# A graph network on one core: each gather asks SyncE and waits for its answer to the one before

## The reference

```python
h = relu(layernorm(x)); x = x + L0(h)   # 4 heads: softmax over a node's edges of (k[src]*q[dst]), typed weights, 8 edge types
h = relu(layernorm(x)); x = x + L1(h)   # GAT: softmax of leaky_relu(a_src[src] + a_dst[dst]), then a feed-forward part
h = relu(layernorm(x)); x = x + L2(h)   # graph convolution: agg = segment_sum(h[src], dst)
h = relu(layernorm(x)); x = x + L3(h)   # 8 heads: exp(clip(k[src]*q[dst], -5, 5)), sums over dst, a feed-forward part
```

## Time and profile before

| | us |
|---|---|
| median of 3 runs (lowest, highest) | 12209.15 (12207.96, 12222.4) |
| profiled execution, its own time | 12230.88 |
| its span in the trace | 12229.1 |
| windows taken for the four passes | 534 to 3580, 3774 to 6710, 6922 to 9181, 9340 to 12070 |

### The profile page before, as it was taken

One profiled execution on the slowest core, in us unless ns is written; L12 is line 12 of the kernel. 1 busy time (PEld: TensorE's weight loads), 2 busy tenths in 40 slices (PEclk: granted clock), 3 DMA queues, 4 the chain that ended last, 5 costly groups with the idle time before them and its releaser, 6 DMA issues. The chain is left out here.

```text
span 12229.1 us, 162378 instructions
## 1 busy us (share of the span) xinstructions
PE 7123.3 (58%) x41810; PEld 5769.1 (47%) x41811; DVE 4523.4 (37%) x12921; ACT 2930.1 (24%) x7688; POOL 6254.5 (51%) x6407
## 2 busy tenths in 40 slices
PE   5766666666665555555555433333335666666667
PEld 3555555555553444444444333222233555555555
DVE  4244444444454444444444411111113333333334
ACT  1233333333333333333333300000002211212112
POOL 1244444444543555555554466666663555555552
PEclk9866566665666555555555655556555665666667
DMA  3322222222221111111111122222222222222221
GB/s 116 134 69 66 68 70 67 69 70 68 69 61 41 38 37 38 38 37 38 37 38 36 42 46 46 46 46 47 46 46 64 76 76 74 77 77 76 75 76 49
DMA packets 379359, 730.33 MB, mean 60 GB/s; under 512 B 169738, under 2 KB 219201, under 8 KB 372838
## 3 DMA queue, kind: packets, MB, share of 16 engines
q0 software_dynamic: 251264, 621.88, 19.5%
q1 hardware_dynamic: 100474, 96.66, 2.4%
q10 hardware_dynamic: 27500, 10.39, 0.4%
HBM read 651.60 MB, written 76.88 MB: 60 GB/s over the span
## 5 line engine op out<-in xcount | busy, mean ns | idle before, releaser
L461 POOL DMA_INDIRECT edges_rows<-kv_typed,edges_idx_r x1568 | 1505.5, 960 | 1584.1 <-DVE edges_wv L781 1103.1
L461 POOL DMA_INDIRECT edges_rows<-gat_rows,edges_idx_r x1568 | 1523.3, 971 | 1421.3 <-DVE edges_wv L781 985.6
L461 POOL DMA_INDIRECT edges_rows<-kv_rows,edges_idx_r x1568 | 1516.6, 967 | 1237.5 <-DVE edges_wv L1145 775.7
L461 POOL DMA_INDIRECT edges_rows<-conv_rows,edges_idx_r x1568 | 1544.5, 985 | 777.0 <-issue 456.9
L609 PE MATMUL edges_ps_sum<-edges_wv,edges_pick 128*128 128x132 f32 x7040 | 1733.5, 417 | 96.5 <-issue 91.0
L985 PE MATMUL edges_ps_sum<-edges_rows,edges_pick 128*128 x3520 | 768.1, 356 | 1516.9 <-issue 1388.5
L609 PEld LDWEIGHTS edges_ps_sum<-edges_wv,edges_pick 128*128 128x128 f32 x7040 | 1466.0, 302 | 268.6 <-issue 246.8
L985 PEld LDWEIGHTS edges_ps_sum<-edges_rows,edges_pick 128*128 128x128 f32 x3520 | 648.9, 258 | 1636.1 <-issue 1634.5
L1083 PE MATMUL edges_ps_q<-q,edges_pick_t 128*128 x3520 | 799.1, 401 | 918.7 <-ACT edges_pick_t L1121 727.8
L1083 PEld LDWEIGHTS edges_ps_q<-q,edges_pick_t 128*128 128x128 f32 x3520 | 728.9, 305 | 968.5 <-issue 968.5
L591 PE MATMUL edges_ps_q<-q,edges_pick_t 128*128 x3520 | 821.9, 409 | 563.9 <-ACT edges_pick_t L696 429.5
(11 more groups left out here) (344 smaller groups left out, 11299.7 us busy)
## 6 DMA issues: line engine op xcount, KB each, us to landing
kv_typed<-l0pre_out SPq DMA_DIRECT2D x49, 1024.0 KB
edges_rows<-kv_typed,edges_idx_r POOLq DMA_INDIRECT x1568
edges_rows<-gat_rows,edges_idx_r POOLq DMA_INDIRECT x1568
edges_rows<-conv_rows,edges_idx_r POOLq DMA_INDIRECT x1568
edges_rows<-kv_rows,edges_idx_r POOLq DMA_INDIRECT x1568
edges_feat_r<-visit_features ACTq DMA_DIRECT2D x660, 10.0 KB
kv_rows<-l3pre_kv SPq DMA_DIRECT2D x7, 896.0 KB, 4.0
edges_flag_r<-visit_flags ACTq DMA_DIRECT2D x220, 16.0 KB
```

Source lines behind the costliest of these rows:

```text
L461: pool.indirect_dma_start(rows[:, k, g * width:(g + 1) * width], None, table, bass.IndirectOffsetOnAxis(ap=idx_r[:, k, g:g + 1], axis=0)). ...
```

## The change

Two semaphores are new, `asked` and `answered`; `slot_free` is gone. Ahead of every gather but the first of a pass POOL waits until `answered` has counted the gather before, and counts `asked` up; the gather follows. SP's stream now runs over the same groups as POOL's, and for each gather waits for `asked` and counts `answered` up. POOL counts `asked` for gather n and issues it without waiting for the answer to n; it is gather n+1 that waits for that. The index lists are loaded from the same loop of SP, after the second group of every 7 (`k % HALF == 1`), with a wait for `rows_ready` of one group more than before.

```diff
-def supply(sp, idx, idx_r, idx_in, rows_ready):
+def supply(sp, idx, idx_r, idx_in, rows_ready, asked, answered):
...
     for n in range(2):
         load(n * HALF, n)
-    with sp.bass.Fori(1, NGP // SLOTS, engines=only(sp), hint_back_edge=True) as it:
-        for n in range(2):
-            sp.wait_ge(rows_ready, (it - 1) * SLOTS + (n + 1) * HALF)
-            load(it * SLOTS + n * HALF, n)
+
+    def body(j, k, it):
+        for g in range(G):
+            sp.wait_ge(asked, j * G + (g + 1))
+            sp.sem_inc(answered, 1)
+        if k % HALF == 1 and known(j, HALF) and (not isinstance(j, int) or j + SLOTS - 1 < NGP + HALF):
+            sp.wait_ge(rows_ready, j - 1)
+            load(j - 1 + HALF, (k // HALF + 1) % 2)
+    groups(sp, body)
...
         if known(j, SLOTS):
             pool.wait_ge(used, at_least_one(pool, visits[k % HALF], NV))
-        pool.sem_inc(slot_free, 1)
         for g in range(G):
+            if g or known(j, 1):
+                pool.wait_ge(answered, j * G + g)
+            pool.sem_inc(asked, 1)
             pool.indirect_dma_start(rows[:, k, g * width:(g + 1) * width], None, table,
                                     bass.IndirectOffsetOnAxis(ap=idx_r[:, k, g:g + 1], axis=0)).then_inc(rows_in[k], 16)
```

More of the change, by code:

```diff
@@ L441, in supply, with fetch @@
         load(n * HALF, n)
-    with sp.bass.Fori(1, NGP // SLOTS, engines=only(sp), hint_back_edge=True) as it:
-        for n in range(2):
-            sp.wait_ge(rows_ready, (it - 1) * SLOTS + (n + 1) * HALF)
-            load(it * SLOTS + n * HALF, n)
-def fetch(nc, pool, res, rows, table, width, idx_r, idx_in, rows_in, rows_ready, used, slot_free):
+    def body(j, k, it):
[6 more added lines that the diff above has]
+    groups(sp, body)
+def fetch(nc, pool, res, rows, table, width, idx_r, idx_in, rows_in, rows_ready, used, asked, answered):
     visits = []
@@ L513, in softmax_pass @@
         rows_in, idx_in = [p.sem(f"rows_in{k}") for k in range(SLOTS)], [p.sem(f"idx_in{k}") for k in range(2)]
-        rows_ready = p.sem("rows_ready")
-        (slot_free, zeroed, squares_done, pick_t_done, pick_tb_done, pick_b_done, pick_done, q_done, prod_done, edge_done,
+        rows_ready, asked, answered = (p.sem(n) for n in ("rows_ready", "asked", "answered"))
+        (zeroed, squares_done, pick_t_done, pick_tb_done, pick_b_done, pick_done, q_done, prod_done, edge_done,
          logit_done, turn_done, run_done, back_done, ends_done, ends_high, ends_low, marked, restarted, top_part, absent_done,
@@ L529, in _ @@
                     sp.dma_start(source[:], idx.rearrange("p g t -> p (g t)")).then_inc(source_in, 16)
-                supply(sp, idx, idx_r, idx_in, rows_ready)
+                supply(sp, idx, idx_r, idx_in, rows_ready, asked, answered)
             @block.gpsimd
             def _(pool):
-                fetch(nc, pool, res, rows, table, width, idx_r, idx_in, rows_in, rows_ready, wv_done, slot_free)
+                fetch(nc, pool, res, rows, table, width, idx_r, idx_in, rows_in, rows_ready, wv_done, asked, answered)
             @block.tensor
@@ L947, in conv_pass @@
         rows_in, idx_in = [p.sem(f"rows_in{k}") for k in range(SLOTS)], [p.sem(f"idx_in{k}") for k in range(2)]
-        rows_ready, slot_free = p.sem("rows_ready"), p.sem("slot_free")
+        rows_ready, asked, answered = (p.sem(n) for n in ("rows_ready", "asked", "answered"))
         local_in, pick_done, sum_done, acc_done = (p.sem(n) for n in ("local_in", "pick_done", "sum_done", "acc_done"))
@@ L963, in _ @@
                 sp.dma_start(local[:], dram["local"]).then_inc(local_in, 16)
-                supply(sp, idx, idx_r, idx_in, rows_ready)
+                supply(sp, idx, idx_r, idx_in, rows_ready, asked, answered)
             @block.gpsimd
             def _(pool):
-                fetch(nc, pool, res, rows, table, aw, idx_r, idx_in, rows_in, rows_ready, sum_done, slot_free)
+                fetch(nc, pool, res, rows, table, aw, idx_r, idx_in, rows_in, rows_ready, sum_done, asked, answered)
             @block.tensor
```

2 lines of the change are left out of this document (1 added, 1 removed).

## The result

The changed kernel takes 12,647.4 us (median of 4 runs, 12,598.5 to 12,656.9) against 12,215.2 for the kernel before: a ratio of 1.0346, 95% interval 1.0317 to 1.0374. Forecast were 11,524 us and a gain.

The account below looks back on a forecast made before the run. Long runs of gathers holding up other engines' signals and sequencers, not work, were taken to bound the passes. 6272 gathers at 1.64 us plus 1258 us gave 11,544, 685 below the span; off the median, 11,524 us, range 10,300 to 12,900.

Parts of the forecast that it names:

- That signals are held while gathers run: In the four edge passes, back-to-back gathers delay other engines' semaphore updates; ACT's L696 waits 1261.8 us in the first pass.
- the prediction's formula: Time is 1258 us outside the edge passes plus 6272 gathers times the time per gather; break-even at 1.749 us.
- POOL slows exactly when signals are held: In the edge passes SP's late answers stop POOL, held signals come through, and answers are quick again; 685 us gained.
- n of about six: Gathers POOL issues before SP's answer comes late: between four and eight, taken as six, giving 1.64 us per gather.
- the gate: POOL's wait for SP's answer ahead of each gather, expected to close in long runs of gathers and ration them.
- The pace p: Time per gather in the edge passes, 1.25 us within a run before; forecast 1.64, gaining below 1.749.
- ACT's wait: Sign in the first pass: ACT L696's wait for "remote" falls from 1262 us to less than half.
- The instructions costed at nothing: POOL's 98 more instructions per 56 gathers hide beside the gather before; 407 us without that cover. SP's cost nothing.
- That a list has cover enough: Index lists load one group later; each serves 28 gathers, at least 35 us, so a 5 us delay costs nothing.
- Over-throttling: Rival: SP's answers are late after three or four gathers or nearly always; 12,736 to 13,990 us; chance one in four.
- The second rival: Consumers advance only while POOL is silent, or answers are never late; passes stay 10,971 us, time 12,209; chance 0.15.
- Instruction fetch mechanics: Rule for SP's loop: in-sequence fetching is hidden, so answers are never late and the time stays at 12,209 us.

Follow-up runs that it names:

- free sets: Two of the six sets of runs, in which the unchanged kernel before took 9300 and 9301 us.
- the repeat of the change: The changed kernel run again unaltered, against the kernel before at 12,015.3 us: 12,416.6 us, ratio 1.0334.
- holding sets: The sets of runs, the result's among them, in which the unchanged kernel before took 12,000 to 12,230 us.

## Why the prediction was wrong

**That signals are held while gathers run** (and with it the reading that work doesn't bound the passes) was right for the sets of the result's kind, and larger than I had put it. That gathers in long runs are enough to hold them was wrong, as the free sets show. Where nothing is held, the same kernel takes 9300 us, not 12,209, close to the 9098 (1258 + 6272 x 1.25) that follow from the prediction's formula at the bare pace of gathers.

**The step that failed** is "POOL slows exactly when signals are held". I took SP's slow instructions as a sign that its answers would be late in runs, with n of about six. In the changed kernel the instruction that answers takes 17 ns in the median, POOL's gathers keep their 1.25 us in the median, and taking the gate out changes nothing (1.0329 against 1.0334). The pace p stayed that of the consumers, so 1258 + 6272 p with p = 1.64 had no footing. Runs of gathers did not become shorter by a gate either (in the third pass they did, but without it just as much: 143 starts more than 2 us apart, 142 in the repeat of the change); in the first pass the pauses are still pauses for a slot, and ACT's wait is 1213 us where I had asked for less than half of 1262.

**The instructions costed at nothing** is the step that decided the sign. I let 98 more on POOL per 56 gathers lie beside the gather before, priced them at 37 ns and 407 us if the cover failed, and gave SP's 112 a turn no price at all since nobody waits for them. The cover did fail in the third pass, where the gap inside a group grew by 0.11 us, with the gate (0.42) and without it (0.41). Elsewhere cover was the wrong question: in holding sets the added instructions of SP and POOL cost 17 to 22 ns each on average, and SP's have no gather to delay. The 21,904 of the change cost 401 us in the set with its repeat (12,416.6 - 12,015.3), which is 18 ns each. The same reasoning gave `slot_free` no worth; the kernel without it, and with `rows_ready` later, is 0.4% faster. That a list has cover enough held in the change, and failed once SP had eight counts per group.

**The rivals.** Over-throttling was the one on the slower side and gave 12,736 us, near the 12,647 measured, but by a mechanism that the runs exclude. The second rival (answers never late, only silence counts) had the mechanism nearly right, the gate that doesn't act, and the time at 12,209, for want of a price for instructions. The rule of the Trainium skill, "Runtime: NRT & Kernel Launch", section "Instruction fetch mechanics", by which the fetching of code that runs in sequence is hidden, was the better guide to whether the gate closes. What the added instructions cost is another matter: nothing in the free sets, 0.15% per 1000 in the holding ones.

**What the gate would have done if it closed** was only tried in free sets, where it costs 39%. Whether it would pay where signals are held stays open.

**Also open** is what an instruction and a held signal compete for. Shown is that the price is there for counts and drains on SP, off every other engine's stream, and for POOL's waits and counts, and that it vanishes with the holding for SP's and ACT's instructions. For ACT, and for the checks, an instruction's own time would do. All added instructions stand in the passes with gathers, so what they would cost outside isn't known. What differs between the sets wasn't in my hand, and no run here names the shared resource.

## What to carry to other kernels

Where a profile shows engines idle for "remote" or "issue" beside long runs of gathers, count instructions, not only waits: here 1000 of them on SP and POOL cost 0.14 to 0.18% while signals were held, though hidden, and leaving out unread counts and run-time checks gave 1.2%. An engine that nobody seems to wait for still has a task; see that it has time for it once its stream is longer. A handshake that is to throttle an engine must be late by itself; one that is answered in the shadow of the work it guards gates nothing and only adds instructions. And when a releaser's name changes from one kernel to the next with the idle time nearly as before, look in a timeline whether it is the same wait.

## What was not expected of the hardware

The same program took 12,000 to 12,230 us in some sets of runs and 9300 in others, each time alike in all its executions. In the free sets the gathers of a pass follow one another at 1.26 to 1.31 us, and an ALU instruction of SP in the third pass takes 39 ns at the longest; in the holding set with the same kernel it takes up to 1397 ns. Eight counts per group on SP were 4.3% in the one kind and 0.01% in the other (the change itself was only run in holding sets), so a timing of such a kernel says little without the time of the kernel before beside it.
